# Second routing in three parts: tiles normalized on GpSimd instead of ScalarE, output pairs ahead of the router's groups, one reciprocal instead of four

## The reference

```python
x = x + 0.5 * ffn(layernorm(x), Wg, W_in, W_out)
x = x + attention(layernorm(x), Wq, bq, ..., Wo, bo, J_attn, lambda_attn)
x = x + 0.5 * ffn(layernorm(x), Wg, W_in, W_out)

def ffn(x, Wg, W_in, W_out):            # 4096 tokens, 8 experts, top 2, capacity 1280
    probs = softmax(x @ Wg)
    top_vals, top_idx = top_k(probs, 2)
    loc = running count of earlier choices of the same expert
    gates = top_vals * (loc < C), divided by their sum
    hid = einsum('ech,ehf->ecf', the tokens of each expert, W_in); a, g = split(hid, 2)
    out_e = einsum('ecf,efh->ech', gelu(a) * g, W_out)
    return sum over the two choices of gate * out_e

def attention(x, ...):
    scores = Q K^T / 4 + lambda * (tanh(Q) J) tanh(K)^T, causal
    return (softmax(scores) V) Wo^T + bo
```

## Time and profile before

| | |
|---|---|
| runs (us) | 1685.26, 1690.79, 1694.33 |
| median (us) | 1690.79 |
| the profiled execution's own time (us) | 1685.26 |
| its span (us) | 1683.5 |
| its mean granted TensorE clock | 0.932 of full speed |
| busy: TensorE, weight load, VectorE, ScalarE, GpSimd (us) | 1468.1, 1084.1, 1026.8, 705.7, 687.1 |

### The profile page before, as it was taken

One profiled execution on the slowest core, in us unless ns is written; L12 is line 12 of the kernel. 1 busy time (PEld: TensorE's weight loads), 2 busy tenths in 40 slices (PEclk: granted clock), 3 DMA queues, 4 the chain that ended last, 5 costly groups with the idle time before them and its releaser, 6 DMA issues. The chain is left out here.

```text
span 1683.5 us, 25093 instructions
## 1 busy us (share of the span) xinstructions
PE 1468.1 (87%) x8708; PEld 1084.1 (64%) x8708; DVE 1026.8 (61%) x2570; ACT 705.7 (42%) x1095; POOL 687.1 (41%) x633
## 2 busy tenths in 40 slices
PE   5389999999735799999999999989865899999994
PEld 2278888998734455555555555445534888888884
DVE  6655555555355577777777778865365556555651
ACT  3233333333222145655656566555532333333331
POOL 1145566554331443333333332234204355656533
PEclk9689999999957689999999999999986999999997
DMA  8334544443257936665667566472163344444525
GB/s 277 107 96 97 100 102 100 95 93 48 32 174 216 260 105 171 173 167 159 173 161 185 152 191 209 128 189 85 56 221 92 71 98 98 80 80 97 99 32 131
DMA packets 125838, 218.77 MB, mean 130 GB/s; under 512 B 20256, under 2 KB 86304, under 8 KB 122592
## 3 DMA queue, kind: packets, MB, share of 16 engines
q1 hardware_dynamic: 89104, 166.09, 34.4%
q0 software_dynamic: 30720, 42.62, 15.8%
q10 hardware_dynamic: 5904, 8.66, 1.8%
HBM read 131.08 MB, written 90.18 MB: 131 GB/s over the span
## 5 line engine op out<-in xcount | busy, mean ns | idle before, releaser
L1855 ACT ACTIVATE a_wts<-a_s_psum 128x1024 f32<-128x1024 f32 (+1 forms) x384 | 301.0, 810 | 185.2 <-PE a_s_psum L1972 183.0
L785 POOL DMA_INDIRECT sums<-e_res,e_sum_row x160 | 259.5, 1622 | 290.3 <-ACT e_res L906 263.5
L1731 DVE CUSTOM_DVE_ANT_0 a_m_psum<-a_m_psum,mask 128x128 f32<-128x128 f32 (+3 forms) x512 | 249.1, 502 | 135.0 <-PE a_m_psum L1947 127.1
L1947 PE MATMUL a_m_psum<-a_kp,a_qp 96*128 96x512 f32 (+2 forms) x768 | 290.0, 412 | 29.8 <-DVE a_parts L1731 9.8
L1947 PEld LDWEIGHTS a_m_psum<-a_kp,a_qp 96*128 96x128 f32 x768 | 149.5, 197 | 149.3 <-DVE a_parts L1731 60.2
L236 POOL DMA_INDIRECT e_slots<-normalized,e_token x160 | 167.0, 1044 | 182.1 <-DVE e_token L528 128.6
L894 ACT ACTIVATE e_act_a<-e_a_psum 128x512 f32<-128x512 f32 (+1 forms) x192 | 101.1, 528 | 288.6 <-PE e_a_psum L970 252.6
L1679 POOL TENSOR_SCALAR_AFFINE_SELECT a_wts<-a_wts 128x512 f32<-128x512 f32 x128 | 78.4, 638 | 337.0 <-ACT a_wts L1855 337.0
L828 DVE TENSOR_TENSOR e_hid<-e_act_a,e_g_psum 128x512 f32<-128x512 f32 (+1 forms) x192 | 114.6, 597 | 161.4 <-PE e_g_psum L970 134.0
L1972 PE MATMUL a_s_psum<-a_qp,a_kp 97*128 97x512 f32 (+2 forms) x768 | 210.2, 356 | 0.4 <-ACT a_wts L1855 0.2
L987 PE MATMUL e_o_psum<-e_w_hi,e_h_hi 128*128 128x256 f32 x640 | 182.9, 286 | 0.0
(11 more groups left out here) (258 smaller groups left out, 2495.5 us busy)
## 6 DMA issues: line engine op xcount, KB each, us to landing
packs<-x_res SPq DMA_DIRECT2D x48, 512.0 KB, 5.9
e_w_raw<-in_W_in SPq DMA_DIRECT2D x16, 1024.0 KB, 8.5
a_qp<-packs SPq DMA_DIRECT2D x16, 1024.0 KB, 7.7
a_kp<-packs SPq DMA_DIRECT2D x16, 1024.0 KB, 13.4
e_w_raw<-in_W_out SPq DMA_DIRECT2D x16, 512.0 KB, 8.5
normalized<-r_xn SPq DMA_DIRECT2D x16, 512.0 KB, 4.9
sums<-x_res SPq DMA_DIRECT2D x2, 4096.0 KB, 16.7
x_res<-sums SPq DMA_DIRECT2D x8, 1024.0 KB, 12.1
```

What stands on the lines that cost most here:

```text
L785: nc.gpsimd.indirect_dma_start(sum_dram, bass.IndirectOffsetOnAxis(ap=sum_row[:, at:at + 1], axis=0), res[j][:], None, bounds_check=last_r ...
L1731: nc.vector.tensor_tensor_reduce(products, products, c["mask"][:, QC - width:], 1.0, MASKED, ALU.add, ALU.max, top).then_inc(max_read, 1)
L1855: nc.scalar.activation(wts[(u * NS + s) % 2][:, j, 0:w], s_ps[q % 2][:, 0:w], ACT.Exp).then_inc(weighed, 1)
L1947: nc.tensor.matmul(m_ps[bank((n, h, z))][:, 0:stream], qp[n % NB][0:PACK, h, qt * P:(qt + 1) * P], kp[n % NB][0:PACK, h, part * QC:part * ...
```

## The change

`HALVES` of the tail, which says in what parts the tiles are normalized, becomes three: tiles 0 to 15, 16 to 23 and 24 to 31. GpSimd normalizes the first two parts, the first ahead of its two averages and the second behind them; VectorE normalizes the third. ScalarE normalizes nothing, and the vector `shift` goes. VectorE computes variances and deviations of part 1 as soon as the first four pairs are in. SyncE no longer waits for the averages before it loads the weights of the first expert. TensorE does all of pairs 4 to 7 behind the transposes of group 1. Groups 0 to 5 share one transpose bank, group 6 has the other and group 7 the first. ScalarE's copies are in another order, exponential 0 stands behind the copy of group 6. In `attend` the four reciprocals become one at place 10 of group 12.

```diff
@@ -302,7 +302,7 @@
     U = NT // CH
     PIECES = 4
     N = NK // PIECES
-    HALVES = [slice(0, U), slice(U, NT)]
+    HALVES = [slice(0, U), slice(U, NT)] if r == 0 else [slice(0, IN_ATTENTION), slice(IN_ATTENTION, TAIL), slice(TAIL, NT)]
     with ExitStack() as ctx:
         sb = lambda n, s, dt=F32: kit.sb(f"r{r}_{n}", s, dt, ctx)
         ps = lambda n, s: kit.ps(f"r{r}_{n}", s, ctx)
@@ -339,8 +339,7 @@
             NY, PAIRS = len(y_at), SEQ // P // 2
             PER_HALF = PAIRS // 2
             assert NY == PAIRS
-            tp = [tp[0]] * (G // CH) + [tp[1], tp[0]] * (G // CH // 2)
-            shift = sb("shift", [P, U])
+            tp = [tp[0]] * (TAIL // 4) + [tp[1], tp[0]]
             sums_in, inverted, inv_out, averaged, y_done, y_read, deviated = kit.sems(
                 "p", "sums_in inverted inv_out averaged y_done y_read deviated")
             o_in = kit.sems("p_o_in", "0 1")
@@ -365,7 +364,6 @@
                     sp.wait_ge(inv_out, 16)
                     for z in range(2):
                         load_inverses(sp, tail["inv"][z], tail["inv_dram"], ALL_HALVES - 2 + z, KD - 1, o_in[z])
-                    sp.wait_ge(averaged, 2)
                 load_weights(nc.sync, held, w_in_dram, w_out_dram, 0, w_loaded)
                 for q in range(NT // 4):
                     sp.wait_ge(normed, (q + 1) * 4)
@@ -384,11 +382,19 @@
                 link = chain(kit, pool, "pool_step")
                 if r == 0:
                     build_constants(kit, c, pool, link)
+                def normalize(tiles, part):
+                    pool.wait_ge(deviated, part + 1)
+                    for t in range(NT)[tiles]:
+                        nc.gpsimd.tensor_scalar(xn[:, t * D:(t + 1) * D], x[:, t * D:(t + 1) * D], mean[:, t:t + 1],
+                                                rstd[:, t:t + 1], ALU.subtract, ALU.mult).then_inc(normed, 1)
+
                 if tail:
+                    normalize(HALVES[0], 0)
                     for z in range(2):
                         pool.wait_ge(o_in[z], 2 * 16)
                         nc.gpsimd.tensor_tensor(tail["mean"][z][:, KD - 1, :], tail["mean"][z][:, KD - 1, :],
                                                 tail["inv"][z][:, KD - 1, :], ALU.mult).then_inc(averaged, 1)
+                    normalize(HALVES[1], 1)
                 nc.gpsimd.memset(gates[:], 0.0).then_inc(gates_clear, 1)
                 link(nc.gpsimd.iota(number_i[:], pattern=[[1, NK]], base=1, channel_multiplier=0))
                 nc.gpsimd.tensor_copy(number[:], number_i[:].unsqueeze(2).to_broadcast([P, NK, 2])).then_inc(numbered, 1)
@@ -428,14 +434,17 @@
                     dve.wait_ge(sums_in, 16)
                     nc.vector.reciprocal(divisors[:], divisors[:]).then_inc(inverted, 1)
                     deviations(HALVES[0], 0)
-                    nc.vector.scalar_tensor_tensor(shift[:], mean[:, HALVES[0]], -1.0, rstd[:, HALVES[0]], ALU.mult, ALU.mult).then_inc(deviated, 1)
-                    for z in range(2 * PAIRS // PER_HALF):
-                        add_pairs(z * PER_HALF, PER_HALF)
-                    dve.wait_ge(stats_done, NT - IN_ATTENTION)
-                    variances(HALVES[1])
-                    deviations(HALVES[1], 1)
-                    dve.wait_ge(normed, IN_ATTENTION)
-                    normalize(HALVES[1])
+                    dve.sem_inc(deviated, 1)
+                    for part in range(1, len(HALVES)):
+                        for z in range(2):
+                            add_pairs((part - 1) * PAIRS + z * PER_HALF, PER_HALF)
+                        dve.wait_ge(stats_done, part * 2 * PAIRS)
+                        variances(HALVES[part])
+                        deviations(HALVES[part], part)
+                        if part == 1:
+                            dve.sem_inc(deviated, 1)
+                    dve.wait_ge(normed, TAIL)
+                    normalize(HALVES[-1])
                 else:
                     for part, tiles in enumerate(HALVES):
                         for t in range(NT)[tiles]:
@@ -566,11 +575,6 @@
                         act.wait_ge(w_loaded, 32)
                     nc.scalar.copy(held["hi"][0][:, a:b], held["raw"][:, a:b]).then_inc(w_split, 1)
 
-                def normalize(g):
-                    for t in range(g * 4, g * 4 + 4):
-                        nc.scalar.activation(xn[:, t * D:(t + 1) * D], x[:, t * D:(t + 1) * D], ACT.Identity,
-                                             bias=shift[:, t:t + 1], scale=rstd[:, t:t + 1]).then_inc(normed, 1)
-
                 roots(0)
                 if r == 0:
                     for g in range(G):
@@ -586,25 +590,23 @@
                     taken(G - 1)
                     exponentials(1)
                 else:
-                    act.wait_ge(deviated, 1)
-                    normalize(0)
-                    normalize(1)
                     turned(0)
-                    normalize(2)
+                    turned(1)
                     taken(0)
-                    turned(1)
-                    normalize(3)
+                    roots(1)
+                    turned(2)
                     taken(1)
-                    for g in range(2, G // CH):
+                    turned(3)
+                    taken(2)
+                    roots(2)
+                    for g in range(4, TAIL // 4):
                         turned(g)
-                        taken(g)
-                    roots(1)
-                    for g in range(G // CH, G):
-                        turned(g)
-                        if g > G // CH:
-                            taken(g - 1)
-                        if g == G - 2:
-                            exponentials(0)
+                        taken(g - 1)
+                    taken(TAIL // 4 - 1)
+                    turned(G - 2)
+                    exponentials(0)
+                    turned(G - 1)
+                    taken(G - 2)
                     taken(G - 1)
                     exponentials(1)
                     for z in range(len(W_PARTS)):
@@ -662,25 +664,22 @@
                     for v in range(PAIRS):
                         pair(v)
                     transposes(0)
-                    for g in range(G // CH):
+                    logits(0)
+                    transposes(1)
+                    for v in range(PAIRS, 2 * PAIRS):
+                        pair(v)
+                    for g in range(1, TAIL // 4):
                         logits(g)
-                        if g:
-                            turn_back(g - 1)
-                        if g + 1 < G // CH:
+                        if g - 1 == G // CH:
+                            pe.wait_ge(y_read, 2 * PAIRS)
+                        turn_back(g - 1)
+                        if g + 1 < TAIL // 4:
                             transposes(g + 1)
-                        if g < 2:
-                            for v in range(PAIRS + g * PER_HALF, PAIRS + (g + 1) * PER_HALF):
-                                pair(v)
-                    turn_back(G // CH - 1)
-                    pe.wait_ge(y_read, 2 * PAIRS)
-                    transposes(G // CH)
-                    transposes(G // CH + 1)
-                    for g in range(G // CH, G):
+                    transposes(G - 2)
+                    transposes(G - 1)
+                    for g in range(TAIL // 4, G):
                         logits(g)
-                        if g > G // CH:
-                            turn_back(g - 1)
-                        if g + 2 < G:
-                            transposes(g + 2)
+                        turn_back(g - 1)
                 else:
                     transposes(0)
                     transposes(1)
@@ -1457,8 +1456,6 @@
 
         LATER = range(FIRST_LATER, ALL_HALVES)
         HOSTS = 2 * (len(LATER) - 1)
-        INVERT_AT = [10, 12, 14, 16]
-        assert len(INVERT_AT) * P == QC
         BO_FROM, BO_TILES = HOSTS + 1, NT // (GROUPS - HOSTS - 2) // 2
         IN_FIRST = {0: (("x", 0), ("x", 1), ("y", 0, 0), ("y", 0, 1), ("v", 0), ("v", 1), ("v", 2), ("v", 3), ("t", 0)),
                     8: (("y", 1, 0),), 12: (("y", 1, 1),), 40: (("t", 1),)}
@@ -1581,7 +1578,7 @@
                 all_stored(GROUPS - NG)
                 sp.dma_start(sums, of_heads(o_dram)[0:EARLY // 2, HD, :, :]).then_inc(sums_in, 16)
                 next_groups(GROUPS - NG - 1, (GROUPS - NG - 1) % NB)
-                sp.wait_ge(inverted, len(INVERT_AT))
+                sp.wait_ge(inverted, 1)
                 sp.dma_start(inv_dram[0:EARLY, :], sums).then_inc(inv_out, 16)
                 sp.wait_ge(inv_out, 16)
                 for i in range(2):
@@ -1599,7 +1596,7 @@
                 sp.dma_start(divisors, sums_of(o_dram, third)).then_inc(sums_in, 16)
                 for z in range(2):
                     load_attended(sp, tail["mean"][z], o_dram, ALL_HALVES - 2 + z, 0, tail_in[z])
-                sp.wait_ge(inverted, len(INVERT_AT) + 1)
+                sp.wait_ge(inverted, 2)
```

(5 more changed lines are left out.)

## The result

The changed kernel takes 1708.93 us, median of five runs (1704.20 to 1711.21), against 1690.79, also of five (1685.26 to 1694.33): a ratio of 1.0102, 95% interval 1.0074 to 1.0132, so 12.5 to 22.3 us slower. The forecast was 1689.9. The profiled execution took 1705.45 us with a span of 1703.5, 20.0 more than the span before.

What follows compares the result with a forecast made beforehand. The kernel was taken as a series of stages, TensorE busy 87%, bounded by what precedes the second routing's hand-over. Attention -5.55 plus routing +4.7 gave -0.85 us: median 1689.9 us, range 1681 to 1699.

Steps and rivals of the forecast that it cites:

- the upper bound of a GpSimd tile: Second routing, normalization moved to GpSimd: at most 0.75 us a tile, adding 3.2 us; as a rival, chance 0.18.
- The value I took, 0.5: Second routing: GpSimd normalizes a tile in 0.5 us, 16 in 8 us, hidden behind TensorE.
- the threshold from which the kernel would be slower, 1.1 us a tile: Second routing: only from 1.1 us a GpSimd tile on would the kernel be slower by 8.5 us.
- The step's own formula: Second routing: 16 tile times plus 1.27 for the first average, from 1207.5, against TensorE ready for pair 4 at 1217.6.
- The order, +4.7: Second routing: new TensorE and ScalarE order spaces logits 5.0 us apart against 4.35; choose(1) starts 4.7 us later.
- The stall, -6.25: End of attention: earlier inverses let averages' transfers start earlier, so TensorE's whole wait for values and its low clock go, -6.25 us.
- the rival of a larger stall: End of attention: other runs' excess is the same wait, so the change gains 6.4 to 10 us; chance 0.17.
- The block, +0.7 (0 to 2.0): End of attention: the 3.4 us reciprocal on VectorE stops TensorE about 2.1 us, against 1.41 before: +0.7 us.
- The low clock in the chain, 0.08: Rival, second routing: TensorE's clock stays low through groups 1 to 7, +16 us, 1706.7; chance 0.08.

Runs made afterwards that it cites:

- the first one after: The first profiled execution of the changed kernel, unaltered: 1705.45 us, where the median of its five runs is 1708.93.
- the one with ScalarE's tiles: Changed kernel with tiles 0 to 15 normalized by ScalarE again, GpSimd making averages first, then tiles 16 to 23: 1697.93 us, ratio 0.9998.
- the kernel of the forms: Changed kernel with GpSimd's 16 instructions on tiles 0 to 15 in eight forms, two tiles each, values wrong: 1697.47 us, run only once.
- the two kernels with 4.35: Logits copy put first in groups 2 to 5: changed kernel with ScalarE's tiles, 1686.56 us; changed kernel with averages behind tile 7 and four early reciprocals, 1692.37.

## Why the prediction was wrong

**The step that failed is the upper bound of a GpSimd tile, "From above: its tensor_tensor takes 1.270 for 512 columns where VectorE's takes 0.69, a ratio of 1.85, and VectorE's own normalization takes 0.405, so 0.75."** It measured 1.209, three times VectorE's 0.405. The bound carried a ratio of two engines over from one kind of instruction to another, and on GpSimd the kind decides: at 256 columns tensor_tensor takes 0.60, less than the barest tensor_scalar. The value I took, 0.5, started from a cast, and by the copy's 0.39 and the cast's 0.61 for 512 columns that is of the cheap kind. The Trainium skill, "GPSIMD Engine Reference", section 3.1, measured its 1.96 on an addition of two tensors; the trace agrees for that kind (1.85), and neither a row nor that section had a tensor_scalar. An operation that no row shows had in truth no upper bound, and the threshold from which the kernel would be slower, 1.1 us a tile, was in the text without a chance of its own.

The step's own formula holds with the right duration: 16 x 1.209 + 1.27 + 1207.5 - 1217.6 = +10.5. Counted from the routing's start it puts pair 4 at 24.4 us, and 24.40 is measured, against 13.70 in the earlier trace rows. Of these 10.7 us 9.67 are the wait, and most of the rest is the first four pairs, which took 9.51 us for 8.67 because more of them ran at the low clock. What the formula left out is that TensorE starts again at the low clock after such a wait: +2.4 for the two pairs. 4.2 for the order, 10.7 and 2.4 make 17.3, as measured. It is shown, not only argued: the new order without GpSimd's tiles is +4.2, GpSimd's tiles without the new order are +14.7.

**The order, +4.7:** right. +4.2 alone, with the period at 4.90 for 5.0, and 4.35 once the copies are swapped. From logits 5 to choose(1), the exponential between, it is 10.7 us (1257.95 to 1268.61) for 10.6 worked out.

**The stall, -6.25:** right, -5.9 in the profile. Its cause, transfers that queue late, is shown by moving only the reciprocals (21.29 and no wait). The profiled execution had the smallest stall of those seen: the windows 27.54, 29.31 and 31.07, with waits of 4.66 to 7.23 us, belong to the same code of the attention. So the rival of a larger stall was partly true as well, and hidden under the loss.

**The block, +0.7 (0 to 2.0):** the wait was sized right (2.31 for 2.1); the sum was not. Measured is 26.01 - 22.70 = +3.3, over its bound. The bound left out that the clock falls behind the wait (0.50 from 1084 to 1086), an estimated 1.7 us beside the wait. Had the four reciprocals only been moved, neither would be paid in this window: 11.2 us gained for 4.7.

**The low clock in the chain, 0.08:** too small. Logits stood 4.90 apart in six profiled executions. In two of them (the first one after, and the one with ScalarE's tiles) the clock held; in the four others it fell for one group (65.27, and the kernel of the forms), two (55.42) or three (69.62), at 1.3 to 1.6 us each. In the two kernels with 4.35 it held. It is part of why the runs of this order scatter.

**Sum.** One reciprocal measures -4.7 and the routing's rows +17.3: +12.6. The changed kernel measured +17.2 (12.5 to 22.3) and +15.4 (12.4 to 18.5); the groups at low clock, 1.2 to 5.5 us a run, are of the size of the difference, which no run shows to be their doing. The 12.6 lies just inside the lower end of both intervals.

## What to carry to other kernels

Price an instruction by rows of its own kind on its own engine; where there is none, say that the cost has no upper bound and work out from what duration on the forecast turns over, then give that side its due chance. When a transfer is late, move the small operation that feeds it earlier before making it larger: a long one blocks the engine and stops another. After a stop of TensorE such as the 2.3 and the 9.7 us here, add what the lower clock costs to the wait itself. Even the 0.86 us stop of an early reciprocal brought the clock down in one execution.

## What the hardware showed beside this

- GpSimd's tensor_scalar has a price of its own: 1.21 us for 128x256 with two operands a row, 1.06 with two constants, 0.84 with one, beside 0.60 for tensor_tensor and 0.39 for a copy.
- The same stop of 1.66 us in every 4.90 left the granted clock at 1.00 in two executions and brought it down in four others for one to three groups. What decides it no run here shows.
- While GpSimd worked on its tiles, some small operations of VectorE lasted up to 0.49 us, and others kept their 0.17, as in the two rows below of VectorE's timeline after. The same operations on the next eight tiles, when GpSimd is done (from 1240.49), take 0.17 each. The Trainium skill, "SBUF — State Buffer", section "Who interferes with whom", says that a VectorE instruction with two inputs in SBUF contends with a GpSimd instruction that reads SBUF, and that their shared ports are an exclusive lock. By that rule, the trace agrees that they contend, but not with a lock for a whole instruction: GpSimd's, 1.2 us each, stood one right behind another, and an operation of VectorE that takes 0.17 us alone lost 0.32 at most. It cost nothing here, since the chain ran through GpSimd.

```profile
1217.39 0.17 DVE L193 TENSOR_TENSOR r_tmp<-r_tmp 128x8 f32<-128x8 f32 x1
...
1218.07 0.49 DVE L196 SCALAR_TENSOR_TENSOR r_tmp<-r_tmp 128x8 f32<-128x8 f32 x1
```
